# A linear cross-attention and ternary feed-forward kernel: the order of keys, queries and first attention of the last batch pair

## The reference

```python
def heads(x, W, b, S): return (x @ W.T + b).reshape(B, S, 16, 32).transpose(0, 2, 1, 3)
q, k, v = heads(layernorm(x), Wq, bq, 256), heads(ctx, Wk, bk, 256), heads(ctx, Wv, bv, 256)
q_prime = relu(einsum('bhnd,fd->bhnf', q, Wqf))          # 64 features
k_prime = relu(einsum('bhnd,fd->bhnf', k, Wkf)) * mask
kv      = einsum('bhnf,bhne->bhfe', k_prime, v)
out     = einsum('bhmf,bhfe->bhme', q_prime, kv) / (q_prime . sum_n k_prime + 1e-8)
x = x + out @ Wo.T + bo
# then, on layernorm(x) quantised to 8 bits, with ternary w_gate, w_up, w_down:
x = x + down(quant(subln(up * square(relu(gate)))))
```

## Time and profile before

| | |
|---|---|
| median of 3 runs | 437.4 us (436.38 to 437.67) |
| profiled execution | 437.74 us, of it 435.7 us from the first to the last instruction |
| busy share of that span | PE 97%, DVE 79%, ACT 66%, POOL 34%, PEld 66% |
| mean granted clock of TensorE | 0.992 of 2.4 GHz |

### The profile page before, as it was taken

The page is one execution under the profiler, slowest core; times in us unless marked ns, Lnnn a source line. Parts: engine busy times, 40 slices in busy tenths (PEclk is TensorE's granted clock), DMA queues, the critical chain, the costliest instruction groups (busy, mean ns, idle before and its releaser), DMA issues.

```text
span 435.7 us, 10242 instructions
## 1 busy us (share of the span) xinstructions
PE 420.6 (97%) x4323; PEld 288.7 (66%) x4323; DVE 342.4 (79%) x505; ACT 287.3 (66%) x406; POOL 146.5 (34%) x290
## 2 busy tenths in 40 slices
PE   8999999999999699999999999999999999999995
PEld 5788789889996574764575575477457567464443
DVE  4634919529953887998997898899998898898983
ACT  5765969766126248778728674963974887948970
POOL 0000000003531371553464425646216443434560
PEclk9999999999999699999999999999999999999999
DMA  7991734605500200033024032312303120333055
GB/s 230 418 410 57 295 144 171 266 2 196 194 3 27 96 18 9 2 62 77 33 49 98 2 72 52 47 48 64 62 24 62 38 48 14 71 88 62 13 116 150
DMA packets 51166, 42.36 MB, mean 97 GB/s; under 512 B 43056, under 2 KB 44080, under 8 KB 49200
## 3 DMA queue, kind: packets, MB, share of 16 engines
q1 hardware_dynamic: 51120, 41.70, 31.9%
HBM read 27.01 MB, written 4.19 MB: 72 GB/s over the span
## 4 chain that ended last, share of the span: by engine, by line
PE 65%; DVE 15%; ACT 6%; POOL 6%; issue 5%; DMA 2%; DVEq 0%; POOLq 0%; ACTq 0%
PE ps L352 54%; DVE zb L358 3%; PE ps L581 3%; PE ps L554 3%; DVE rows_of L364 3%; PE ps L676 2%; POOL tk L361 2%; ACT rb L355 2%; DVE tk L760 2%; PE ps L653 1%; ACT kT L355 1%; POOL zb L358 1%; DMA xqT<-xqb 1%; PE ps L615 1%; DVE rows_of L358 1%
## 5 line engine op out<-in xcount | busy, mean ns | idle before, releaser
L352 PE MATMUL ps<-tg,xqT 128*128 128x512 bf16 x256 | 60.6, 380 | 0.7 <-DMA xqT<-xqb 0.6
L352 PE MATMUL ps<-tu,xqT 128*128 128x512 bf16 x256 | 60.6, 380 | 0.2 <-DVE zb L358 0.2
L361 POOL TENSOR_SCALAR tk<-tk 128x1 f32<-128x1 f32 x96 | 38.1, 398 | 38.2 <-DVE tk L711 20.6
L352 PE MATMUL ps<-td,yqT 128*128 128x512 bf16 x208 | 46.9, 380 | 0.0
L352 PEld LDWEIGHTS ps<-tu,xqT 128*128 128x128 bf16 x256 | 24.2, 98 | 31.1 <-issue 2.1
L355 ACT ACTIVATE rb<-zb 128x1024 f32<-128x1024 f32 x29 | 30.6, 1056 | 20.9 <-DVE zb L358 20.8
L352 PEld LDWEIGHTS ps<-tg,xqT 128*128 128x128 bf16 x256 | 23.5, 98 | 30.7 <-issue 2.4
L358 DVE TENSOR_TENSOR zb<-ps,rb 128x1024 f32<-128x1024 f32 x29 | 35.3, 1217 | 5.3 <-ACT rb L355 5.2
L352 PE MATMUL ps<-aph,wqh 128*128 128x256 f32 x128 | 37.2, 291 | 0.0
L760 DVE TENSOR_REDUCE tk<-zb 128x1 f32<-128x1024 f32 x30 | 36.2, 1207 | 1.0 <-POOL zb L358 0.8
L352 PE MATMUL ps<-apl,wkh 128*128 128x256 f32 x128 | 35.2, 279 | 1.0 <-issue 1.0
(11 more groups left out here) (130 smaller groups left out, 1063.4 us busy)
## 6 DMA issues: line engine op xcount, KB each, us to landing
xs<-in_wg_dram SPq DMA_DIRECT2D x4, 1024.0 KB, 13.7
xs<-in_wu_dram SPq DMA_DIRECT2D x4, 1024.0 KB, 6.6
xs<-in_wd_dram SPq DMA_DIRECT2D x4, 1024.0 KB, 7.4
xs<-in_x_dram SPq DMA_DIRECT2D x8, 512.0 KB, 4.4
out_dram<-xs SPq DMA_DIRECT2D x15, 256.0 KB, 2.1
craw<-in_ctx_dram SPq DMA_DIRECT2D x7, 512.0 KB, 7.3
xs<-in_wk_dram SPq DMA_DIRECT2D x4, 256.0 KB, 4.2
xs<-in_wv_dram SPq DMA_DIRECT2D x4, 256.0 KB, 6.1
```

Source lines behind the costliest of these rows:

```text
L352: return add("pe", name, cost, waits, lambda e: e.matmul(out, lhsT, rhs, start=start, stop=stop))
L361: return add(lane, name, cost, waits, lambda e: e.tensor_scalar(out, a, s1, s2, op0, op1))
```

## The change

The words of the first FLOW line are put in another order. `X0`, `X1`, the query matmuls `W0`, the query features `Q0` and the attention `A0` of pair 0 now stand among the value matmuls of pair 7, directly behind features(6). Keys, kv(6) and features of the last pair (`K7 P6 F7`) stand behind A0. `X2` moves ahead of `S0`, and `P7` from ahead of S0 to behind it. No instruction is added or removed.

Two buffers change with it. Keys of pair 7 are evicted into `kT_last`, a name for the place that was reserved as `low0` (it lies under the first half of `aph`), and not into `kT`. Queries of pair 0 are evicted into `xn`, and not into `kT`.

```diff
 FLOW = (
-    "K7 X0@4 P6 X1@5 F7 V0.4 V4.12 W0.1@7 L1 W0.0@6 V12.18 Q0@0123 V18.24 A0@0123 P7 S0@6 X2@7 X3@4 S1@5 W1.0@6 W1.1@7",
+    "X0@6 V0.4 X1@7 V4.8 V8.12 L1 V12.18 W0.0@6 W0.1@7 Q0@0123 V18.24 A0@0123 K7 P6 F7 X2@5 S0@4 P7 X3@4 S1@5 W1.0@6 W1.1@7",
...
-            upper.enter_context(nc.sbuf_tensor("low0", [P, 1024], F32))
+            kT_last = upper.enter_context(nc.sbuf_tensor("kT_last", [P, 1024], F32))
...
+        def kT_of(b):
+            return kT_last if b == NB - 1 else kT
+
+        def qT_of(a):
+            return qT if a else xn[:, :, :].rearrange("p t c -> p (t c)")
...
-[act(f"kT{b}.{z}.all", 0.4, [k, "small"], kT[:, T * z:T * z + T], outs[z], ACT.Identity, bias=bk[:, z:z + 1]) for z in oqs]
+[act(f"kT{b}.{z}.all", 0.4, [k, "small"], kT_of(b)[:, T * z:T * z + T], outs[z], ACT.Identity, bias=bk[:, z:z + 1]) for z in oqs]
...
-left, right = fkr[rows, weights:weights + 64], (qT if a else kT)[rows, T * q:T * q + T]
+left, right = fkr[rows, weights:weights + 64], qT_of(a)[rows, T * q:T * q + T]
```

More of the change, by code:

```diff
@@ L517, in keys @@
                     oqs = (oq,) if first else (oq - 1, oq)
-                    bank_user[banks[oq]] = [act(f"kT{b}.{z}.all", 0.4, [k, "small"], kT[:, T * z:T * z + T], outs[z], ACT.Identity, bias=bk[:, z:z + 1]) for z in oqs]
+                    bank_user[banks[oq]] = [act(f"kT{b}.{z}.all", 0.4, [k, "small"], kT_of(b)[:, T * z:T * z + T], outs[z], ACT.Identity, bias=bk[:, z:z + 1]) for z in oqs]
         def values(b, t):
@@ L551, in features @@
                             o = T * q + P * t + 64 * c
-                            left, right = kT[32 * r:32 * r + 32, o:o + 64], fkr[32 * r:32 * r + 32, 64 * r:64 * r + 64]
+                            left, right = kT_of(b)[32 * r:32 * r + 32, o:o + 64], fkr[32 * r:32 * r + 32, 64 * r:64 * r + 64]
                             out = ps[64 * c:64 * c + 64, r, 256 * t + 64 * q:256 * t + 64 * q + 64]
@@ L639, in s2 @@
                         k = products(f"qT{a}.{oq}.{kc}", 0.1077, waits, out, (wqh[:, kc, ws], wql[:, kc, ws]), (aph[:, cs], apl[:, cs]), kc == 0, kc == KC - 1)
-                bank_user[b] = [act(f"qT{a}.{oq}.all", 0.4, [k, "small"], (qT if a else kT)[:, T * oq:T * oq + T], ps[:, b, 256 * (oq % 2):256 * (oq % 2) + 256], ACT.Identity, bias=bq[:, oq:oq + 1]) for oq in (2 * o2, 2 * o2 + 1)]
+                bank_user[b] = [act(f"qT{a}.{oq}.all", 0.4, [k, "small"], qT_of(a)[:, T * oq:T * oq + T], ps[:, b, 256 * (oq % 2):256 * (oq % 2) + 256], ACT.Identity, bias=bq[:, oq:oq + 1]) for oq in (2 * o2, 2 * o2 + 1)]
         def s3(a):
```

## The result

The changed kernel takes 432.29 us (median of 4 runs, 430.77 to 432.51), before 437.07 (4 runs, 436.38 to 437.67): a ratio of 0.9884, 95% interval 0.9856 to 0.9912. On a second chip it was measured once more beside the experiments: 432.48 against 438.39, ratio 0.9857 (0.9843 to 0.9871). Ratios and intervals are those of the fast runs alone, and the one slow run, of 1068.05 us with the queries in `kT`, is left out of the median of that kernel too. The forecast was 432.0, with a range from 430.8 to 435.0.

A forecast was written before the change was run, and what follows sets the result against it. PE, busy 97% of the span, was taken as the bound, with a 4.8 us wait at S0. Terms -4.80 - 1.97 + 0.45 + 0.4 + 0.1 + 0.4 = -5.4 gave 432.0 us, range 430.8 to 435.0.

The forecast's parts named there:

- The forecast case: Whole kernel: the terms sum to -5.4 us, median 432.0 us; chance 0.62 for 431 to 433.3.
- The wait at S0: PE's wait ahead of S0 for the attention's chain goes in full, covered by K7, P6, F7 and X2: -4.80 us.
- The clock: At S0: without the wait the granted clock no longer falls, so S0 takes 2.83 in place of 4.80 us: -1.97.
- Q0: New wait within Q0 for the evictions of the last query matmul: +0.45 us, between 0.2 and 0.84.
- F7: New wait at F7 for ACT's eviction kv6.1, no longer hidden under X1: +0.4 us, between 0.28 and 0.7.
- P7: Possible wait at P7 for kf7.rows, behind ln0.12.bst and load x6 on DVE: +0.1 us, between 0 and 0.8.
- S1, W1 and G0.0: Wait at G0.0 for xqT0, its chain 11.5 against 11.0 us of PE work: +0.4 us, between 0 and 1.5.
- the slower one: Rival: x6 lands late, P7 waits 5.0 us and the clock falls again: +1.45, 438.9 us; chance 0.04.
- Lost later: Rival: DVE, not PE, sets the pace after Z0, so the gain need not arrive: 437.4 us; chance 0.08.
- The second wait: Rival: waits at P7, G0.0 and Q0 reach their upper bounds, sum -3.2: 434.2 us; chance 0.22.

The follow-up runs named there:

- the filled wait: The kernel before the change with 20 matmuls of unused results put on PE between P7 and S0: 435.8 us against 438.39, ratio 0.9934.
- x6 late: The changed kernel with the same lists, but load x6 issued only when xn3 is done: 438.45 us against 438.39 before the change, ratio 1.0.

## Why the prediction was right

The forecast case came, with -5.64 us in the stretch of the first profile and -5.26 in that of the second, against a sum of -5.4; the medians fell by 4.8 us on the first chip and 5.9 on the second. DVE's rows in the first profile of the change, for oT0.0.lo, xn2, ln0.12.bst and xT3.lo:

```profile
135.24 0.68 DVE L365 SCALAR_TENSOR_TENSOR qol<-xn,qoh 128x512 fp32r<-128x512 f32 x1
136.03 0.55 DVE L362 TENSOR_SCALAR xn<-xs,mv,rstd 128x512 f32<-128x512 f32 x1
...
138.64 0.70 DVE L606 BATCH_NORM_STATS2 st<-xs 128x6 f32<-128x512 f32 x1
...
146.43 0.68 DVE L359 TENSOR_TENSOR apl<-ps,aph 128x512 fp32r<-128x512 f32 x1
```

The terms, each as a difference of starts, before against the first profile of the change:

- **The wait at S0**, -4.80, gone as a whole. oT0.0.lo now ends at 135.24 + 0.68 = 135.92, 2.6 us ahead of S0, and xn2 at 136.03 + 0.55 = 136.58, 1.5 ahead of X2, where about 2 were given. The cover is made by what the change puts there: with the keys in `kT` the chain ends too late, and with P7 ahead of S0 PE waits at P7 in its place.
- **The clock**, -1.97 in the sum; S0 now takes 2.85 in place of 4.80, -1.95. Shown as a loss of its own by the filled wait.
- **Q0**, +0.45 in the sum: 1.61 in place of 1.04 to the next start, +0.57. The place and the cause were right, shown by the values put ahead of it.
- **F7**, +0.4: 138.08 - 136.11 = 1.97 in place of 1.56, +0.41. In ACT's timeline kv6.1 ends at 136.54, 0.43 behind F7's start, which fits; no run takes this wait away.
- **P7**, +0.1 with a bound of 0.8: a term with the wrong size. P7 comes 0.43 after the last matmul of S0 (0.27 of it shown as a wait) in the first profile, and waits 0.84 in the second and 0.85 with the queries in `kT`, both just over the bound. The time at which PE wants P7 was right: it could have started at 141.34, 13.83 after the denominator (dy0.0 at 127.51 on ACT), with 13.8 given. DVE was late: Wo.lo1 was done and x6 issued at 135.34, 7.83 after the denominator and not about 7.25, and x6 took 3.3, 3.6 and 3.9 us to land in these three; ln0.12.bst starts when it lands (138.64 in the first).
- **S1, W1 and G0.0**, +0.4: the other term with the wrong size. 152.72 - 144.17 = 8.55 in place of 8.51, +0.04. The wait at G0.0 did not come: xqT0 was issued at 150.04 and took 2.5 us (2.7 before), so it landed at 152.54, ahead of G0.0 at 152.72. xm0 took 1.50, as expected beside xbo4 (0.55 + 0.76 by the row of xn3, and 0.2 more), but PE met it at W1: xT3.lo stands behind xm0 and ended at 147.11, and W1 began at 147.16, 0.16 later than S1's end alone would have let it. From there to G0.0 it was 5.56 us in place of 5.68, which gave most of that back; why is not shown.
- **Not in the sum**: X0, X1, the first 18 value matmuls and W0 take 122.64 - 111.83 = 10.81 us; before, X0, X1 (0.53 and 0.58) and the 10.03 from F7's end to Q0 were 11.14. So 0.33 less where nothing had been counted; the rest is within 0.1 each.

So Q0 and P7 cost 0.45 more than in the sum, and 0.69 came back from the last two points. The total hit better than its parts, and that it did is luck: a late P7 and a G0.0 without a wait offset each other.

Of the rivals, the slower one has the mechanism that was given, and turns somewhat earlier (+0.50 with a landing 7.0 behind Wo.lo1); it did not come because x6 lands as early as before. "Lost later" did not come: the 276 us behind G0.0 stayed as they were, and what an experiment won or lost in the stretch shows in its time: the two differ by 0.1 to 1.0 us, the times against 438.39 and the stretches against 48.05. The second wait came in part: P7's at its bound, G0.0's not at all.

On the rule of the Trainium skill (SBUF — State Buffer, section "SBUF: two separate sides"), the exclusive lock of VectorE and GpSimd on a port pair: xm0 was issued at 145.00, just behind POOL's xbo4 (144.93 to 146.22), and ended 0.28 after it, at 146.50, as xn3 did behind xbo2 before the change. With xbo4 put elsewhere it took 0.55. So it was held for nearly the whole of xbo4, as the rule says; the price stayed near the row's, since this xbo4 took 1.29 us and not the 1.66 of xbo2.

## What to carry to other kernels

A wait of the busiest engine can cost more than its own length: read the granted clock behind it, and price the work that runs at the low level from the same work at the high one. To fill such a wait with real work, look first at which buffer ties that work to the chain (here one place that keys and attention shared), and at what the moved work itself waits for. A step that waits for a transfer, put ahead of others in an engine's list, lends its wait to all of them; that is where a reordering can lose everything that it has won.

## What the runs showed of the hardware that was not expected

After a wait the low level of the clock did not last equally long in all kernels. Before the change, S0's large matmuls began at 145.46 and the clock was full from about 149.68, 4.2 us later. With x6 late, the small matmuls of P7 began at 146.52, and it took to about 152.1 (windows of that kernel):

```profile
150.00:152.00 2.00, 2.00 (x11) 1.74 (x10) 0.92 (x1) 0.88 (x2) 1.76 (x3) 0.50 0.00 0
152.00:154.00 2.00, 2.00 (x10) 1.68 (x9) 1.28 (x2) 0.00 (x0) 0.25 (x1) 0.97 0.01 4
```

That is 5.6 us of work at 1.2 GHz, where S0's 4.2 had been the measure for what I expected of the experiments. With P7 ahead of S0 the low level lasted 5.7 us from the start of P7, with the keys in `kT` 5.9 from the start of X2, by the windows of these kernels. These two came out longer than expected by 2.0 us (0.8 of it the wait at X3) and 0.7; x6 late came out at the upper end. Why the low level lasted longer there is not shown.

The first 110 us vary between profiles although their order is the same in all: features(6) began at 110.31 in the first profile of the change, 111.1 to 111.7 in the others, and 113.77 with the queries in `kT`. In the list of waits this shows in part as holes of PE for which the profile shows no releaser ("issue"): 1.7 + 1.0 us in the profile of before, about 0.6 in the first of the change. That first profile, of a run of 430.77 us, lies 1.5 us under the median of its kernel. What these holes are was not tested.
